# Widening in four float16 products in the convolution steps, one float32 strip buffer, and the first statistics ahead of the sign weights

## Chip, cores and metric

The kernel runs on one core of a Trainium2 chip. The metric is device time in microseconds, from the first to the last instruction of the execution, including the little around it. All products run on TensorE (PE), elementwise work on VectorE (DVE), ScalarE (ACT) and GpSimd (POOL); SyncE (SP) issues the transfers.

## What is computed

The input is 32 images of 64 channels and 112x112 pixels, float32. Two layers follow each other; each adds to x the result of a branch whose input is a group normalisation of x (32 groups of 2 channels, no affine part):

```python
# layer 0
x = x + conv3x3(group_norm(x), sign(weight) * alpha)        # 64 -> 64 channels
# layer 1
h = einsum('oc,bchw->bohw', w_in, group_norm(x))            # widening, 64 -> 256 channels
f = rfft2(patches_8x8(h)) * fft_filt;  h = irfft2(f)        # filter in each 8x8 patch
h = depthwise_conv3x3(h, w_dw)
x1, x2 = split(h, 2)                                        # 128 channels each
x = x + einsum('oc,bchw->bohw', w_out, gelu(x1) * x2)
```

## The kernel before

**Tiling.** Two images form a pair and fill the 128 partitions (2 x 64 channels), so there are 16 pairs. A pair is cut into 14 strips of 8 rows. A strip has 14 patches of 8x8, taken two at a time as 7 blocks of 16 columns (`NBLK`). The blocks are worked on in the four groups of `GROUPS`, (0,2), (2,4), (4,6) and (6,7): groups 0 to 2 have two blocks, group 3 has one.

**Layer 1, a strip.** `normalise_patches` (ACT) makes `xn`; `transposed` (PE) and `pixels` (ACT) make `xT`; `forward_transform` (PE) takes the patches to their spectrum, and `spectrum` (ACT) puts it back into the same buffer (`xf = xT`, float32). `widened` (PE) multiplies each block's spectrum with `win_sb` into two PSUM banks, in float32: four 64x64 quadrants a block, 256 columns each. `filtered` (DVE) multiplies by the filter into `hf`. `evaluated` (PE, float32) takes `hf` to 121 nodes of a short convolution scheme, `weighted` (DVE) multiplies by the taps into `v32`. `high_nodes` (ACT) rounds `v32` to float16 (`v_hi`), `low_nodes` (GpSimd) makes the remainder `v_lo` in float16, and `interpolated` (PE, float16) sums both into `Y`. `gelu`, `carried0`, `gated`, `keep0` and `keep1` finish the rows, `projected` (PE) multiplies by `w_out`, and `lifted` (ACT) and `residual` (GpSimd) add it to x.

**Layer 0, a strip.** `stats_x` (DVE) takes the statistics. Once they are complete, `strip32` (ACT) writes the normalised strip in float32 to `n32`, `strip16` (ACT) writes it again in float16 to `S_hi`, a ring of four strips, and `low_strip` (GpSimd) subtracts both into `S_lo`. `convolution` (PE, float16) needs the strips j-1 to j+1 and runs 9 taps x 2 parts x 4 quadrants for half a strip each. `convolved` (DVE) adds the result to x and `stats_1` takes the statistics for layer 1.

**Order.** All five queues are written out by hand in `image(n, ...)`, over 14 steps t. Step t brings the front of strip t (patches, transform, spectrum), widening to nodes of strip t-1, interpolation of strip t-2 and projection of strip t-3, all of pair n, while layer 0 of pair n+1 runs in between: its statistics in steps 0 to 4, its strips' normalisation as `NORM_STEPS` says (strip 0 in step 5, two strips in each of steps 6 to 11, one in step 12), and two convolutions in each of steps 6 to 12. Steps 6 to 12 are the "convolution steps" and have an order of their own; the others are "plain". `kind(b, s)` tells for a strip s of pair b which of the two orders its middle part meets; it is "conv" for strips 5 to 11 of each pair but the last, so in 15 x 7 = 105 cases. In a convolution step `widened` is issued for the groups 1, 3, 0 and 2 (`HF_ORDER`). Before the first `image` the layer 0 of the first pair runs alone: statistics, all 14 strips, all 14 convolutions.

**Waits.** Engines meet at counting semaphores. Those that matter here: `pool_slo` counts finished `low_strip`, and convolution j waits for j+2 of the pair; `pe_conv` counts convolutions, and a slot of the ring is written for strip j once convolution j-3 is done (`act.wait_ge(pe_conv, n * STRIPS + j - RING_STRIPS + 2)`); `act_xf` counts finished `spectrum`; `pool_vlo` guards the four slots of `v32`. In a convolution step ScalarE's queue has, in this order: `gelu` of image 0, `lifted` 0, `strip32(a)`, `keep0`, `lifted` 1, `strip16(a)`, `strip32(b)`, `strip16(b)`, `high_nodes` of image 0, group 3, and so on. GpSimd's has `low_strip(a)`, `residual` 0, `low_nodes(0, 3)`, `low_strip(b)`, `residual` 1, the three other `low_nodes` of image 0, then the four of image 1. Here a and b are the two strips of `NORM_STEPS[t]`. Before, `strip32` takes one of two buffers and waits for the `low_strip` of two strips earlier:

```python
if j >= 2 or not first:
    act.wait_ge(pool_slo, n * STRIPS + j - 1 if j >= 2 else n * STRIPS)
```

Of the kernel before, what the change touches and what calls it, by code (L numbers as in the profile page):

```python
# [8 lines left out]
ALU = mybir.AluOpType  # L9
# [85 lines left out]
def build(nc, x, conv_w, alpha, w_in, w_dw, filt, w_out, forward, pick, pair, identity, nodes, taps, ext, out):  # L95
# [34 lines left out]
    with ctx:  # L130
# [12 lines left out]
        win_sb = sb("win_sb", [128, C2])  # L143
        wout_sb = sb("wout_sb", [HC, C])
# [10 lines left out]
        xf = xT  # L155
        hf = sb("hf", [BPX, IMGS, NBLK, C2])
        v32 = sb("v32", [128, 4, 2, 2, C2])
# [61 lines left out]
        dve_conv = sem("dve_conv")  # L219
        dve_hf = sem("dve_hf")  # L220
# [41 lines left out]
        def kind(b, s):  # L262

            last = isinstance(b, int) and b == PAIRS - 1
            return "conv" if CONV_FROM <= (s + MID) % STRIPS <= CONV_TO and not last else "plain"

# [52 lines left out]
        def _(pool):  # L319
# [13 lines left out]
            def low_strip(n, j):  # L333
                row = j % RING_STRIPS * ROWS
                pool.wait_ge(act_shi, n * STRIPS + j + 1)
                nc.gpsimd.tensor_tensor(S_lo[:, row:row + ROWS, 1:1 + W], n32[:, j % 2],  # L336
                                        S_hi[:, row:row + ROWS, 1:1 + W], ALU.subtract).then_inc(pool_slo, 1)

            def low_nodes(b, s, img, grp):
# [3 lines left out]
                nc.gpsimd.tensor_tensor(v_lo[:, img, :, k0:k1, :], v32[:, V_ORDER[kind(b, s)][img].index(grp), :, 0:k1 - k0, :],  # L343
# [9 lines left out]
            def image(n, par, prev, front, more):  # L353
                for t in range(STRIPS if front else OUT):
                    mid = item(n, t, MID, prev, front)
                    done = item(n, t, OUT, prev, front)
                    if more and CONV_FROM <= t <= CONV_TO:
# [19 lines left out]
                    else:  # L377
# [10 lines left out]
                        if mid:  # L388
# [24 lines left out]
        def _(act):  # L413
            def strip32(n, par, j, first):

                if j == 0:
                    act.wait_ge(dve_grpx, n * 4 + 4)
                if j >= 2 or not first:
                    act.wait_ge(pool_slo, n * STRIPS + j - 1 if j >= 2 else n * STRIPS)
                nc.scalar.activation(n32[:, j % 2], X[par][:, j * ROWS:(j + 1) * ROWS, :], ACT.Identity, bias=nbx[:],  # L420
                                     scale=rstdx[:])

            def strip16(n, par, j, first):

                row = j % RING_STRIPS * ROWS
# [4 lines left out]
                nc.scalar.activation(S_hi[:, row:row + ROWS, 1:1 + W], X[par][:, j * ROWS:(j + 1) * ROWS, :], ACT.Identity,  # L430
                                     bias=nbx[:], scale=rstdx[:]).then_inc(act_shi, 1)
# [10 lines left out]
            def pixels(n, s, bank):  # L442
                act.wait_ge(pe_xT, n * STRIPS + s + 1)
                if n or s:
                    act.wait_ge(pe_hf, 4 * (n * STRIPS + s))
                nc.scalar.activation(xT[:].rearrange("p k c -> p (k c)"), flat(bank, NBLK * 128), ACT.Copy).then_inc(act_xT, 1)  # L446
# [7 lines left out]

            def high_nodes(b, s, img, grp):
# [6 lines left out]
                nc.scalar.activation(v_hi[:, img, :, k0:k1, :], v32[:, V_ORDER[kind(b, s)][img].index(grp), :, 0:k1 - k0, :],  # L462
# [30 lines left out]
            def image(n, par, prev, front, more):  # L493
                for t in range(STRIPS if front else OUT):
# [3 lines left out]
                    if more and CONV_FROM <= t <= CONV_TO:  # L498
# [4 lines left out]
                        if more and len(NORM_STEPS.get(t, ())) > 0:  # L503
                            strip32(n + 1, 1 - par, NORM_STEPS[t][0], False)
# [35 lines left out]
                    else:  # L540
# [20 lines left out]
                        if front:  # L561
                            spectrum(n, t, BANK_P)
                        if mid:
                            high_nodes(mid[0], mid[1], 1, 3)
                        if more and len(NORM_STEPS.get(t, ())) > 0:
                            strip32(n + 1, 1 - par, NORM_STEPS[t][0], False)
                            strip16(n + 1, 1 - par, NORM_STEPS[t][0], False)
# [14 lines left out]
            act.wait_ge(pool_zero, N_ZERO)  # L582
            for j in range(STRIPS):
                strip32(0, 0, j, True)
                strip16(0, 0, j, True)
# [8 lines left out]
        def _(dve):  # L594
# [72 lines left out]
            def weighted(b, s, img, grp, bank):  # L667
# [3 lines left out]
                    v32[:, V_ORDER[kind(b, s)][img].index(grp), :, 0:k1 - k0, :],  # L671
# [26 lines left out]
            def image(n, par, prev, front, more):  # L698
                for t in range(STRIPS if front else OUT):
# [9 lines left out]
                    if more and CONV_FROM <= t <= CONV_TO:  # L709
# [4 lines left out]
                        if mid:  # L714
# [3 lines left out]
                            if before:  # L718
                                dve.wait_ge(pool_vlo[1], 4 * i - 3)
                            weighted(b, s, 0, 3, BANK_Q)  # L720
                            if before:
                                dve.wait_ge(pool_vlo[1], 4 * i - 2)
                            weighted(b, s, 0, 0, BANK_P)
                            if before:
                                dve.wait_ge(pool_vlo[1], 4 * i - 1)
# [3 lines left out]
                        if mid:  # L729
                            if before:  # L730
                                dve.wait_ge(pool_vlo[1], 4 * i)
# [7 lines left out]
                        if mid:  # L739
                            dve.wait_ge(pool_vlo[0], 4 * i + 1)  # L740
# [3 lines left out]
                        if mid:  # L744
                            dve.wait_ge(pool_vlo[0], 4 * i + 2)
# [3 lines left out]
                        if mid:  # L749
                            dve.wait_ge(pool_vlo[0], 4 * i + 3)  # L750
# [3 lines left out]
                        if mid:  # L754
                            dve.wait_ge(pool_vlo[0], 4 * i + 4)
                            weighted(b, s, 1, 0, BANK_P)
                    else:
# [16 lines left out]
                        if mid:  # L774
                            if before:
                                dve.wait_ge(pool_vlo[1], 4 * i - 3)
                            weighted(b, s, 0, 3, BANK_P)
                            if before:
                                dve.wait_ge(pool_vlo[1], 4 * i - 2)
# [5 lines left out]
                        if mid:  # L785
                            if before:
                                dve.wait_ge(pool_vlo[1], 4 * i - 1)
# [427 lines left out]
```

## Time and profile before

| | |
|---|---|
| median of 3 runs | 5393.75 us (5391.17 to 5396.26) |
| the profiled execution, its own time | 5396.35 us |
| its span | 5394.6 us |
| granted TensorE clock, mean | 0.997 |
| busy: PE, DVE, POOL, ACT | 97%, 86%, 79%, 65% |
| PE weight loads | 57% |
| DMA queues | about 11% of 16 engines |

The profile is of one execution. Busy shares are means over two kinds of step, so they are only a first hint; rows of a timeline give an instruction's start and length in microseconds, and in brackets how long the engine was idle before it and which instruction released it. "x40" is a run of 40 records of one kind; a float32 product has two records, a float16 product one. Rows of the chain name the work that held up the end, one after the other. ACT and DVE rows overlap by some 0.1 us, since the next instruction starts before the last one's end is recorded.

### The profile page before, as it was taken

What the parts mean: (1) busy time and instruction counts of PE and PEld (TensorE: products, weight loads), DVE (VectorE), ACT (ScalarE), POOL (GpSimd) and SP (SyncE); (2) the same over time, 40 slices, a digit from 0 to 9 for tenths busy, and PEclk for the clock granted to TensorE, in tenths of its full rate; (3) what the DMA queues carried; (4) which work ended last, traced back from release to release, by engine and by line L of the source; (5) the groups of instructions that cost most, each with busy time, mean ns of one, the idle gap of its engine ahead of it and who ended that gap; (6) DMA issues with size and microseconds to landing.
All of it is one profiled execution on the core that took longest, in us unless ns stands there. A gap on an engine that the chain in (4) does not pass through costs nothing.

```text
span 5394.6 us, 200882 instructions
## 1 busy us (share of the span) xinstructions
PE 5249.1 (97%) x88932; PEld 3061.1 (57%) x88932; DVE 4631.7 (86%) x5701; ACT 3526.7 (65%) x4642; POOL 4236.2 (79%) x2503
## 2 busy tenths in 40 slices
PE   5999999999999999999999999999999999999998
PEld 4555555555555555555555555555555555555554
DVE  6889888898888888888898888988889888898886
ACT  3666666666666666666666676666666667666665
POOL 3878778787887877878778787887878878787787
PEclk9999999999999999999999999999999999999999
DMA  2011010110101101010010100101011110110000
GB/s 103 19 50 43 37 45 28 54 40 37 54 22 50 43 37 53 19 58 35 37 53 28 51 33 38 55 36 43 33 50 40 39 41 33 50 43 20 23 26 26
DMA packets 43804, 219.20 MB, mean 41 GB/s; under 512 B 5350, under 2 KB 5960, under 8 KB 36808
## 3 DMA queue, kind: packets, MB, share of 16 engines
q1 hardware_dynamic: 42952, 206.36, 9.9%
q8 instruction: 716, 11.73, 0.9%
q14 instruction: 136, 1.11, 0.1%
HBM read 103.58 MB, written 102.76 MB: 38 GB/s over the span
## 4 chain that ended last, share of the span: by engine, by line
PE 86%; DVE 10%; issue 3%; DMA 0%; ACT 0%; POOL 0%; DVEq 0%; SPq 0%; POOLq 0%; ACTq 0%
PE PS L913 28%; PE PS L931 21%; PE PS L873 14%; PE PS L901 12%; PE PS L945 7%; DVE v L670 5%; PE PS L882 4%; DVE hf L663 3%; DVE bn L601 1%; DVE g L695 1%; DVE PS L679 0%; DVE PS L686 0%; DMA alpha_sb<-in_alpha 0%; POOL v_lo L343 0%; PE PS L847 0%
## 5 line engine op out<-in xcount | busy, mean ns | idle before, releaser
L343 POOL TENSOR_TENSOR v_lo<-v,v_hi 128x1024 f16<-128x1024 f32 (+1 forms) x1792 | 3357.5, 1898 | 841.9 <-ACT v_hi L462 834.5
L462 ACT ACTIVATE v_hi<-v 128x1024 f16<-128x1024 f32 (+1 forms) x1792 | 1647.0, 944 | 902.4 <-DVE v L670 532.6
L670 DVE TENSOR_TENSOR v<-PS,smul 128x1024 f32<-128x1024 f32 (+1 forms) x1792 | 1909.8, 1086 | 288.6 <-PE PS L913 271.0
L913 PE MATMUL PS<-hf,c_nodes 64*64 64x512 f32 (+1 forms) x14336 | 1661.8, 556 | 25.7 <-DVE v L670 4.5
L931 PEld LDWEIGHTS PS<-c_ext,v_hi 128*128 128x128 f16 x14336 | 1129.9, 97 | 541.2 <-issue 198.5
L931 PE MATMUL PS<-c_ext,v_hi 128*128 128x100 f16 (+2 forms) x14336 | 1258.6, 203 | 5.2 <-ACT gel L482 3.8
L931 PE MATMUL PS<-c_ext,v_lo 128*128 128x100 f16 (+2 forms) x14336 | 1250.2, 202 | 0.0
L931 PEld LDWEIGHTS PS<-c_ext,v_lo 128*128 128x128 f16 x14336 | 1118.0, 97 | 1.2
L663 DVE TENSOR_TENSOR hf<-PS,mult 128x1024 f32<-128x1024 f32 (+1 forms) x896 | 955.0, 1086 | 117.5 <-PE PS L901 101.0
L901 PE MATMUL PS<-win_sb,xT 64*64 64x256 f32 x12544 | 824.9, 388 | 48.0 <-DVE hf L663 28.9
L873 PE MATMUL PS<-S_hi,csign 64*64 64x448 f16 (+2 forms) x8640 | 746.4, 336 | 9.2 <-POOL S_lo L336 9.2
L873 PE MATMUL PS<-S_lo,csign 64*64 64x448 f16 (+2 forms) x8640 | 747.5, 337 | 0.0
L913 PEld LDWEIGHTS PS<-hf,c_nodes 64*64 64x64 f32 x14336 | 407.9, 131 | 583.1 <-DVE v L670 157.0
L901 PEld LDWEIGHTS PS<-win_sb,xT 64*64 64x64 f32 x12544 | 413.7, 132 | 394.3 <-DVE hf L663 160.5
L446 ACT ACTIVATE xT<-PS 128x896 f32<-128x896 f32 x224 | 205.6, 918 | 650.0 <-PE PS L882 650.0
L336 POOL TENSOR_TENSOR S_lo<-n,S_hi 128x896 f16<-128x896 f32 x224 | 411.5, 1837 | 214.6 <-ACT S_hi L430 214.6
L695 DVE TENSOR_TENSOR g<-PS,gel 128x912 f32<-128x912 f32 (+1 forms) x448 | 496.3, 1108 | 58.9 <-DVE PS L686 1.9
L482 ACT ACTIVATE gel<-PS 128x912 f32<-128x912 f32 (+1 forms) x448 | 413.6, 923 | 116.6 <-DVE PS L679 115.6
L945 PE MATMUL PS<-g,wout_sb 128*64 128x448 f32 (+2 forms) x1792 | 445.6, 574 | 7.7 <-DVE g L695 5.9
L873 PEld LDWEIGHTS PS<-S_hi,csign 64*64 64x64 f16 x8640 | 314.1, 107 | 142.8 <-DVE v L670 28.5
L873 PEld LDWEIGHTS PS<-S_lo,csign 64*64 64x64 f16 x8640 | 314.6, 106 | 135.2 <-issue 32.1
L469 ACT ACTIVATE g<-PS 128x448 f32<-128x448 f32 (+1 forms) x448 | 244.7, 546 | 81.3 <-PE PS L945 79.3
(68 smaller groups left out, 4143.2 us busy)
## 6 DMA issues: line engine op xcount, KB each, us to landing
out_x<-Xa SPq DMA_DIRECT2D x96, 448.0 KB, 2.6
out_x<-Xb SPq DMA_DIRECT2D x96, 448.0 KB, 2.5
Xa<-in_x SPq DMA_DIRECT2D x8, 2240.0 KB, 9.0
Xb<-in_x SPq DMA_DIRECT2D x8, 2240.0 KB, 8.9
Xa<-in_x SPq DMA_DIRECT2D x8, 1792.0 KB, 7.0
Xb<-in_x SPq DMA_DIRECT2D x8, 1792.0 KB, 7.2
Xa<-in_x SPq DMA_DIRECT2D x8, 1344.0 KB, 6.0
Xb<-in_x SPq DMA_DIRECT2D x8, 1344.0 KB, 6.4
```

The source lines that it names most:

```text
L336: nc.gpsimd.tensor_tensor(S_lo[:, row:row + ROWS, 1:1 + W], n32[:, j % 2], S_hi[:, row:row + ROWS, 1:1 + W], ALU.subtract).then_inc(pool_s ...
L343: nc.gpsimd.tensor_tensor(v_lo[:, img, :, k0:k1, :], v32[:, V_ORDER[kind(b, s)][img].index(grp), :, 0:k1 - k0, :], v_hi[:, img, :, k0:k1, ...
L462: nc.scalar.activation(v_hi[:, img, :, k0:k1, :], v32[:, V_ORDER[kind(b, s)][img].index(grp), :, 0:k1 - k0, :], ACT.Copy).then_inc(act_vhi ...
L482: nc.scalar.activation(gel[:, :, r0:r1, :], Y[:, :, r0:r1, :], ACT.Gelu).then_inc(act_y0, 1)
L663: nc.vector.tensor_tensor(hf[:, :, k0:k1, :], PS[:, bank:bank + 2, 0:(k1 - k0) * C2].rearrange("p i (k c) -> p i k c", c=C2), mult[:].unsq ...
L670: nc.vector.tensor_tensor(v32[:, V_ORDER[kind(b, s)][img].index(grp), :, 0:k1 - k0, :], PS[:, bank:bank + 2, 0:(k1 - k0) * C2].rearrange(" ...
L695: nc.vector.tensor_tensor(g[:, img, r0:r1, :].rearrange("p r (b c) -> p b r c", c=YC), Y[:, :, r0:r1, :], gel[:, :, r0:r1, :], ALU.mult).t ...
L873: last = nc.tensor.matmul(PS[c * C:(c + 1) * C, bank + h, i0 * W:(i0 + m) * W], csign[r * C:(r + 1) * C, tap, :], S[r * C:(r + 1) * C, row ...
L901: last = nc.tensor.matmul(PS[side * P * P:(side + 1) * P * P, bank + r, (k - k0) * C2:(k - k0 + 1) * C2], xf[r * C:(r + 1) * C, k, side * ...
L913: last = nc.tensor.matmul(PS[points, bank + side, 0:(k1 - k0) * C2], c_nodes[half, points], hf[half, img, k0:k1, :].rearrange("p k c -> p ...
L931: last = nc.tensor.matmul(Y[:, b0, :, col - b0 * YC:end - b0 * YC], v[:, img, patch % 2, patch // 2, half * HC:(half + 1) * HC], c_ext[:, ...
L945: last = nc.tensor.matmul(Z[img * C:(img + 1) * C, 0:(r1 - r0) * HALF_W], wout_sb[:], g[:, img, r0:r1, 1 + q * HALF_W:1 + (q + 1) * HALF_W ...
```

## The change

1. **Widening in convolution steps.** In strips of kind "conv", `spectrum_high` (ACT) rounds the spectrum to float16 right behind `spectrum`, and `spectrum_low` (GpSimd) subtracts it into `xf_lo`. `widened` then uses four float16 products (high x high, low x high, high x low, low x low) that accumulate in PSUM, each with 64 rows (one image) and all 128 columns, 256 columns of result, where it had four float32 quadrants a block. It waits for `pool_xl` in place of `act_xf`. `win_hi` and `win_lo` are made once at the start. In plain steps nothing changes here, except that plain step 5 makes the spectrum of strip 5, which is of kind "conv".
2. **One strip buffer.** `n32` has one slot. `strip16` comes before `strip32` everywhere, and `strip32` waits for the `low_strip` of the strip just before.
3. **Buffers of the nodes.** `v32` has three slots for the groups 0 to 2 and `v31` one small slot of each image for group 3; the counts waited for come from `lows_before`. They are the same numbers as before.
4. **The start.** The statistics of strips 0 to 10 of the first pair stand before the wait for the sign weights, those of 11 to 13 behind it. A small activation into `nb1`, which is overwritten later, runs on ScalarE first.

```diff
-        n32 = sb("n32", [128, 2, ROWS, W])
+        n32 = sb("n32", [128, ROWS, W])
...
+            def spectrum_low(n, s):
+                pool.wait_ge(act_xh, xl_count(n, s + 1))
+                nc.gpsimd.tensor_tensor(xf_lo[:], xf[:], xf_hi[:], ALU.subtract).then_inc(pool_xl, 1)
...
@@ gpsimd, convolution step @@
                             low_nodes(mid[0], mid[1], 0, 2)
+                        if front and kind(n, t) == "conv":
+                            spectrum_low(n, t)
                         if mid:
                             low_nodes(mid[0], mid[1], 1, 3)
@@ gpsimd, plain step @@
                             low_nodes(mid[0], mid[1], 1, 3)
+                        if front and kind(n, t) == "conv":
+                            spectrum_low(n, t)
                         if mid:
                             low_nodes(mid[0], mid[1], 1, 0)
...
@@ scalar @@
             def strip32(n, par, j, first):
+                if j or not first:
+                    act.wait_ge(pool_slo, n * STRIPS + j)
+                nc.scalar.activation(n32[:], X[par][:, j * ROWS:(j + 1) * ROWS, :], ACT.Identity, bias=nbx[:],
+                                     scale=rstdx[:]).then_inc(act_shi, 1)
...
+            def spectrum_high(n, s):
+                i = n * STRIPS + s
+                act.wait_ge(act_xf, i + 1)
+                if i:
+                    act.wait_ge(pe_hf, 4 * i)
+                nc.scalar.activation(xf_hi[:], xf[:], ACT.Copy).then_inc(act_xh, 1)
...
@@ scalar, convolution step @@
-                            strip32(n + 1, 1 - par, NORM_STEPS[t][0], False)
+                            strip16(n + 1, 1 - par, NORM_STEPS[t][0], False)
                         if up:
                             keep0(up[0], up[1], 0)
                         if done:
                             lifted(done[0], done[1], 1)
                         if more and len(NORM_STEPS.get(t, ())) > 0:
-                            strip16(n + 1, 1 - par, NORM_STEPS[t][0], False)
+                            strip32(n + 1, 1 - par, NORM_STEPS[t][0], False)
                         if more and len(NORM_STEPS.get(t, ())) > 1:
+                            strip16(n + 1, 1 - par, NORM_STEPS[t][1], False)
                             strip32(n + 1, 1 - par, NORM_STEPS[t][1], False)
-                            strip16(n + 1, 1 - par, NORM_STEPS[t][1], False)
...
                         if front:
                             spectrum(n, t, BANK_P)
+                            if kind(n, t) == "conv":
+                                spectrum_high(n, t)
...
+            nc.scalar.activation(nb1[:], m_half[:], ACT.Identity)
...
@@ vector, start @@
+            for j in range(STRIPS - 3):
+                stats_x(0, 0, j)
             dve.wait_ge(dma_conv, 16 * N_CONV)
...
-            for j in range(STRIPS):
+            for j in range(STRIPS - 3, STRIPS):
                 stats_x(0, 0, j)
             channels_x(0)
...
+            nc.vector.tensor_copy(win_hi[:], win_sb[:]).then_inc(dve_prep, 1)
+            dve.wait_ge(dve_prep, 3)
+            nc.vector.tensor_tensor(win_lo[:], win_sb[:], win_hi[:], ALU.subtract).then_inc(dve_prep, 1)
...
@@ tensor, widened @@
+                    pe.wait_ge(pool_xl, xl_count(b, s + 1))
+                    for k in range(k0, k1):
+                        for part, (x16, win) in enumerate(((xf_hi, win_hi), (xf_lo, win_hi), (xf_hi, win_lo), (xf_lo, win_lo))):
+                            for r in range(IMGS):
+                                last = nc.tensor.matmul(PS[:, bank + r, (k - k0) * C2:(k - k0 + 1) * C2],
+                                                        x16[r * C:(r + 1) * C, k, :], win[r * C:(r + 1) * C, :],
+                                                        start=part == 0, stop=part == 3)
```

## Rows read from the trace of the kernel before

**Rows 1.** The page: engines' busy time, chain by engine, one group's weight loads.
```profile
PE 5249.1 (97%) x88932; PEld 3061.1 (57%) x88932; DVE 4631.7 (86%) x5701; ACT 3526.7 (65%) x4642; POOL 4236.2 (79%) x2503
...
PE 86%; DVE 10%; issue 3%; DMA 0%; ACT 0%; POOL 0%; DVEq 0%; SPq 0%; POOLq 0%; ACTq 0%
...
L931 PEld LDWEIGHTS PS<-c_ext,v_hi 128*128 128x128 f16 x14336 | 1129.9, 97 | 541.2 <-issue 198.5
```

**Rows 2.** The chain, 2281 to 2309 us: start, length (us), what.
```profile
2283.17 1.38 PE PS L931 x32
2284.55 2.50 PE PS L901 x40
...
2292.93 6.87 PE PS L873 x144
```

**Rows 3.** Timeline, TensorE: start, length (us), instruction, idle time before.
```profile
2285.95 0.64 PEld L901 LDWEIGHTS PS<-win_sb,xT 64*64 64x64 f32 x16 [0.41 <-DVE hf L663]
...
2292.76 0.37 PE L873 MATMUL PS<-S_hi,csign 64*64 64x448 f16 x4
```

**Rows 4.** Timeline of VectorE, same step.
```profile
2296.40 0.68 DVE L644 SCALAR_TENSOR_TENSOR Xb<-PS,alpha_sb,Xb 128x448 f32<-128x448 f32 x1 [1.66 <-PE PS L873]
```

**Rows 5.** Timeline of ScalarE, same step.
```profile
2288.46 1.12 ACT L430 ACTIVATE S_hi<-Xb,nbx,rstdx 128x896 f16<-128x896 f32 x1
2289.48 1.12 ACT L420 ACTIVATE n<-Xb,nbx,rstdx 128x896 f32<-128x896 f32 x1
...
2292.01 1.58 ACT L462 ACTIVATE v_hi<-v 128x512 f16<-128x512 f32 x2 [0.38 <-PE PS L931]
...
2306.03 1.58 ACT L462 ACTIVATE v_hi<-v 128x512 f16<-128x512 f32 x2 [1.54 <-PE PS L931]
```

**Rows 6.** Timeline of GpSimd, same step.
```profile
2280.01 7.55 POOL L343 TENSOR_TENSOR v_lo<-v,v_hi 128x512 f16<-128x512 f32 x4 [1.90 <-ACT v_hi L462]
2289.66 1.84 POOL L336 TENSOR_TENSOR S_lo<-n,S_hi 128x896 f16<-128x896 f32 x1 [2.10 <-ACT S_hi L430]
...
2292.72 1.16 POOL L343 TENSOR_TENSOR v_lo<-v,v_hi 128x512 f16<-128x512 f32 x1 [0.21 <-ACT v_hi L462]
2293.84 1.83 POOL L336 TENSOR_TENSOR S_lo<-n,S_hi 128x896 f16<-128x896 f32 x1
```

**Rows 7.** Timeline of GpSimd, steps 5 and 6 of the same pair.
```profile
2192.66 7.46 POOL L343 TENSOR_TENSOR v_lo<-v,v_hi 128x1024 f16<-128x1024 f32 x4 [1.43 <-ACT v_hi L462]
2201.39 2.14 POOL L343 TENSOR_TENSOR v_lo<-v,v_hi 128x1024 f16<-128x1024 f32 x1 [1.26 <-ACT v_hi L462]
...
2205.27 4.25 POOL L343 TENSOR_TENSOR v_lo<-v,v_hi 128x1024 f16<-128x1024 f32 x2
```

**Rows 8.** Timeline of TensorE, step 6.
```profile
2201.59 1.09 PE L901 MATMUL PS<-win_sb,xT 64*64 64x256 f32 x16 [1.18 <-DVE v L670]
...
2212.27 0.37 PE L873 MATMUL PS<-S_hi,csign 64*64 64x448 f16 x4
```

**Rows 9.** The chain of the first 150 us.
```profile
4.58 15.73 DMA alpha_sb<-in_alpha
...
21.29 14.77 DVE bn L601 x28
...
40.11 1.28 ACT L420
...
45.69 1.84 POOL S_lo L336
...
47.67 50.11 PE PS L873 x980
```

**Rows 10.** Timeline of SyncE's queue, the four loads of the first pair.
```profile
0.74 1.89 SPq L276 DMA_DIRECT2D Xa<-in_x  x4
```

**Rows 11.** DMA issues, first 60 us: first and last of these four, us to landing.
```profile
Xa<-in_x SPq DMA_DIRECT2D x1, 2240.0 KB, 8.2
...
Xa<-in_x SPq DMA_DIRECT2D x1, 1344.0 KB, 17.4
```

More of the change, by code:

```diff
@@ L265, in kind, with xl_count, kind_after, nodes32 @@
             return "conv" if CONV_FROM <= (s + MID) % STRIPS <= CONV_TO and not last else "plain"
+        def xl_count(b, s):
+            return (STRIPS // 2) * b + min(max(s - CONV_FROM + MID, 0), STRIPS // 2) if b < PAIRS - 1 else (STRIPS // 2) * b
+        def kind_after(b, s):
+            return kind(b, s + 1) if s < STRIPS - 1 else kind(b + 1, 0)
+        def nodes32(b, s, img, grp):
+            if grp == 3:
+                return v31[:]
+            return v32[:, [other for other in V_ORDER[kind(b, s)][img] if other != 3].index(grp)]
+        def lows_before(b, s, img, grp):
+            if img == 0:
+                b, s = (b, s - 1) if s else (b - 1, STRIPS - 1)
+            mine, theirs = V_ORDER[kind(b, s) if img else kind_after(b, s)][img], V_ORDER[kind(b, s)][1 - img]
+            if grp == 3:
+                at = theirs.index(3)
+            else:
+                at = theirs.index([other for other in theirs if other != 3][[other for other in mine if other != 3].index(grp)])
+            return 4 * (b * STRIPS + s) + at + 1
         def conv_strips(t):
@@ L335, in low_strip @@
                 pool.wait_ge(act_shi, n * STRIPS + j + 1)
-                nc.gpsimd.tensor_tensor(S_lo[:, row:row + ROWS, 1:1 + W], n32[:, j % 2],
+                nc.gpsimd.tensor_tensor(S_lo[:, row:row + ROWS, 1:1 + W], n32[:],
                                         S_hi[:, row:row + ROWS, 1:1 + W], ALU.subtract).then_inc(pool_slo, 1)
+            def spectrum_low(n, s):
+                pool.wait_ge(act_xh, xl_count(n, s + 1))
+                nc.gpsimd.tensor_tensor(xf_lo[:], xf[:], xf_hi[:], ALU.subtract).then_inc(pool_xl, 1)
             def low_nodes(b, s, img, grp):
@@ L414, in strip32, with strip16 @@
             def strip32(n, par, j, first):
+                if j or not first:
+                    act.wait_ge(pool_slo, n * STRIPS + j)
+                nc.scalar.activation(n32[:], X[par][:, j * ROWS:(j + 1) * ROWS, :], ACT.Identity, bias=nbx[:],
+                                     scale=rstdx[:]).then_inc(act_shi, 1)
+            def strip16(n, par, j, first):
+                row = j % RING_STRIPS * ROWS
                 if j == 0:
                     act.wait_ge(dve_grpx, n * 4 + 4)
[L418 to L425, printed above, removed]
                 if j >= RING_STRIPS:
@@ L461, in high_nodes @@
                     act.wait_ge(pe_y, 4 * i - 2 + 2 * img)
-                nc.scalar.activation(v_hi[:, img, :, k0:k1, :], v32[:, V_ORDER[kind(b, s)][img].index(grp), :, 0:k1 - k0, :],
+                nc.scalar.activation(v_hi[:, img, :, k0:k1, :], nodes32(b, s, img, grp),
                                      ACT.Copy).then_inc(act_vhi[img], 1)
@@ L562, in image @@
                             spectrum(n, t, BANK_P)
+                            if kind(n, t) == "conv":
+                                spectrum_high(n, t)
                         if mid:
@@ L897, in widened @@
                 k0, k1 = GROUPS[grp]
-                pe.wait_ge(act_xf, b * STRIPS + s + 1)
-                for k in range(k0, k1):
-                    for r, side in ((0, 0), (1, 1), (0, 1), (1, 0)):
-                        last = nc.tensor.matmul(PS[side * P * P:(side + 1) * P * P, bank + r, (k - k0) * C2:(k - k0 + 1) * C2],
-                                                xf[r * C:(r + 1) * C, k, side * P * P:(side + 1) * P * P],
-                                                win_sb[r * C:(r + 1) * C, :], start=True, stop=True)
+                if kind(b, s) == "plain":
+                    pe.wait_ge(act_xf, b * STRIPS + s + 1)
+                    for k in range(k0, k1):
+                        for r, side in ((0, 0), (1, 1), (0, 1), (1, 0)):
+                            last = nc.tensor.matmul(PS[side * P * P:(side + 1) * P * P, bank + r, (k - k0) * C2:(k - k0 + 1) * C2],
+                                                    xf[r * C:(r + 1) * C, k, side * P * P:(side + 1) * P * P],
+                                                    win_sb[r * C:(r + 1) * C, :], start=True, stop=True)
+                else:
+                    pe.wait_ge(pool_xl, xl_count(b, s + 1))
+                    for k in range(k0, k1):
+                        for part, (x16, win) in enumerate(((xf_hi, win_hi), (xf_lo, win_hi), (xf_hi, win_lo), (xf_lo, win_lo))):
[3 more added lines that the diff above has]
+                                                        start=part == 0, stop=part == 3)
                 last.then_inc(pe_hf, 1)
```

55 lines of the change are left out of this document (32 added, 23 removed).

## Prediction

> **What bounds the kernel now.** I read the page first: the tensor engine is busy 97% of the span, and the chain that ended last is 86% tensor engine and 10% vector engine [rows 1]. Such a share says nothing yet of one stage, so I then read the chain and the timelines of one convolution step (image pair 6, 2282 to 2309 us). Below I call the groups of the widening W1, W3, W0 and W2 in the order in which a convolution step issues them, and the two strips that a step normalises a and b.
>
> The chain of that step [rows 2] shows three things. The float32 widening of five blocks takes 2.50 us, 0.50 a block. The float16 convolution takes 6.87 us for 144 products, 36 sets of four 64x64 quadrants, 0.19 us a set of 448 columns. That is one set at the pace of one stream (448 columns at 2.4 GHz are 0.187): quadrants with different rows, and quadrants with the same columns and another bank, run beside each other, and the loads cost nothing. The float16 interpolation needs 1.38 us for 32 products with 128x128 weights, 43 ns for a load and a product. So the engine streams nearly without a gap, and what it is given less to do is worth something, unless another engine holds it at that place. Two places are close. W2 begins at 2285.95 and its loads waited for the vector engine's result of W3 [rows 3]. The second convolution of the step begins at 2292.76 + 3.43 = 2296.19 [rows 2, 3], and it needs the low half of strip b, which GpSimd finishes at 2293.84 + 1.83 = 2295.67 [rows 6]: half a microsecond of room.
>
> **The widening itself.** Seven convolution steps in each of 15 pairs, 105 in all, change. Before: seven blocks at 0.50. After: four products of 256 columns for each half of the rows, the halves beside each other. By the conv's rate a pair of streams costs 256/448 of 0.19, which is 0.109 us, and four of them 0.44 a block. Half of the array's rows with all 128 columns is a shape of which the trace has no fast example. From below, 4 x 256 columns at 2.4 GHz are 0.427. From above, nothing beside anything, it is 0.85. I take 0.44, since the quadrants show both kinds of overlap and the 43 ns show 128-column loads hidden. That saves about 0.05 a block. W1 gives 0.10, W3 0.05, which moves the vector engine's filtered W3 and with it W2 by 0.15; W2 gives 0.10 more. So the first projection and all behind it come 0.25 us earlier, not 7 x 0.06 = 0.4, since W0 is done before W2 may start.
>
> The Trainium skill ("TensorE: Matmul & The Clock Gate", Part 3, the mechanism) says that a weight load overlaps products in flight only when its row group differs. By it each of the four rounds would show its load, and the kernel would be slower; the 43 ns above, all on the same rows, speak against it, and it is a rival below.
>
> **Added on ScalarE and GpSimd.** spectrum_high: a 128x896 activation costs at most the 1.12 us of the strip's. It comes behind spectrum, where ScalarE sat idle 1.54 us before v_hi [rows 5]: hidden. spectrum_low: 128x896, float32 less float16, like a strip's 1.84 us [rows 6]. In a convolution step GpSimd was idle 1.90 us before low_nodes(1,3) at 2280.01. It can begin about 1.0 us after spectrum's end, so 1.84 of work in the rest of that gap pushes low_nodes(1,3) by 0.5. Behind it wait four v_lo (7.55 us, to 2287.56) and then low_strip(a), which before waited until 2289.66 [rows 6]: 2.1 us of cover. The vector engine wants these buffers in the next step only: hidden.
>
> **One strip buffer.** strip16(a) takes the place of strip32(a) and the reverse, so low_strip(a) starts when it did. But strip32(b) must now wait for it. From the start of strip32(a), which stands where S_hi stood at 2288.46 [rows 5], I add: 1.12 and 0.08 to GpSimd's start (2289.66), 1.84, a hand-over of 0.07 (an estimate, a little under the 0.08 of the other way), then 1.02 (as from 2288.46 to 2289.48) until ScalarE takes v_hi for group 3, 0.71 from there to GpSimd (2292.01 to 2292.72), 1.12 to the next strip (2292.72 to 2293.84), 1.83, and 0.14 to the tensor engine (45.69 + 1.84 to 47.67). The sum is 7.93 and ends at 2296.39 [rows 5, 6, 9]. The second convolution stood ready at 2296.19, so it would now wait 0.20. (The vector engine's [1.66] wait at 2296.40 [rows 4] is for the first convolution; it has time.) Both sides start 0.25 earlier. A step with two strips so gains 0.25 - 0.20 = 0.05. Bounds: 0.25 where the chain fits, a loss of 0.2 where hand-overs are 0.1 dearer and the widening saves half. Step 12 has one strip and gains the full 0.25.
>
> **The first convolution step of each pair.** The spectrum of strip 5 is made in plain step 5, and its low half is queued behind low_nodes(1,3). That ends at 2192.66 + 7.46 = 2200.12, and GpSimd was idle only 1.26 us until 2201.39 [rows 7]. So spectrum_low runs 2200.12 to 2201.95. W1 waits for it: 2202.05 in place of 2201.59 [rows 8]. low_nodes(1,0) ends 2204.07, low_strip(0) 2205.85, two v_lo (4.2) 2210.05, low_strip(1) 2211.9. Now the single buffer: strip32(2) from 2211.95, v_hi 2212.97, v_lo 2213.68, low_strip(2) 2214.80 to 2216.63, second convolution 2216.77. Before it stood at 2212.27 + 3.43 = 2215.70 [rows 8]. That is 1.07 us late, with the widening's gain swallowed. GpSimd catches up soon after, in idle time like the 1.90 us of [rows 6], so this happens once a pair. Bounds 0.6 to 1.3, by the same hand-overs.
>
> Per pair: 5 x 0.05 + 0.25 - 1.07 = -0.57, which is 8.6 us lost over 15 pairs.
>
> **The start.** The sign weights' work waits until 20.3 us, and the 28 statistics (14.77 us, 1.055 a strip) stand behind it, to 36.06 [rows 9]. The four loads were issued from 0.74 to 2.6 [rows 10] and landed 8.2 to 17.4 us after issue [rows 11]. After: 11 strips from 8.9 to 20.5, sign weights 0.95, three strips 3.2, to 24.6: 11.4 us earlier. The other copies for the filter weights (128x256 each) lie beside the tensor engine's group sums: nothing. The new small activation on ScalarE draws the 1.28 us table load out of the chain [rows 9]. Against it: the first two strips in one buffer are 1.02 + 1.12 + 0.08 + 1.84 + 0.07 + 1.12 + 0.08 + 1.84 + 0.14 = 7.3 us instead of 47.67 - 41.39 = 6.3. And from strip 4 a slot of the ring comes free only when convolution j-2 is done. Then strip16, strip32 and the low half follow, some 4.35 us with the hand-overs, while a convolution takes 3.43 [rows 2]; before, strip32 was ahead, and 3.2 fitted. Convolution j waits for j-2's end + 4.35, so every second one waits 0.9: five, 4.5 us. Sum: -11.4 - 1.3 + 1.0 + 4.5 = -7.2 us, from -9 to -4.
>
> **The sum.** 5394.6 + 8.6 - 7.2 = 5396.0 of span. The profiled execution took 1.75 more than its span and 2.6 more than the median of the three runs, so the forecast is 5395 us. Its own range is 5383 to 5405.
>
> **Rivals.** A, faster: the chain of the single buffer is a little shorter than summed, the convolution never waits for strip b, and blocks cost 0.43. Then 90 steps give 0.3 (27 us), the first step of a pair loses 0.8 (12), the start gives 7: 5372. For it: 0.2 us decides it. Against: every hand-over summed comes from a row. It decides once each two-strip step gains 0.18 instead of 0.05.
> B, slower: the same chain is dearer, as ScalarE takes strip32(b) late and keep1, v_hi and the second strip pile up behind it. At 0.3 us a step in 75 steps: 5395 + 22 = 5417. It decides from 0.13 a step on. For it: four queued instructions are now in series, and each may slip. Against: ScalarE has idle time left, 1.54 us at one place of the step alone [rows 5].
> C, slower by far: the row halves do not run together, 0.85 a block: 0.35 x 7 x 105 = 257 us, 5650. A second way to nearly the same end is that loads are shown: 97 ns of a float16 load [rows 1] and 107 of stream, four times, are 0.82 a block, 0.32 x 735 blocks = 235 us, 5630. This is the skill's rule named above (its section gives no other price here); 43 ns a pair [rows 2] is against it.
>
> **Chances.** Forecast 0.44, A 0.24, B 0.25, C 0.07. 0.2% (11 us) is about what a measurement can tell from no change. Faster 0.24, same 0.44, slower 0.32. The range, 5371 to 5428, takes in A and B and leaves out C and some of the tails.
>
> **What would show it.** Five blocks of widening at 2.2 us in place of 2.5. A wait of the second convolution for S_lo, 0.2 us in most convolution steps and near 1 us in the first of a pair. GpSimd's spectrum_low at 1.84 with W1 of the first step waiting for it. The statistics ending near 24.6 us, the first convolution near 36. I am wrong if a block costs more than 0.5, if no wait for S_lo shows, or if the filtered group 3 no longer gates W2.

## The result and the profile after

| | before | after |
|---|---|---|
| median of 12 runs each | 5393.86 us (5391.17 to 5396.26) | 5406.49 us (5402.29 to 5412.72) |
| profiled execution, own time | 5396.35 us | 5403.27 us |
| its span | 5394.6 us | 5401.2 us |
| PE, DVE, POOL, ACT busy | 97%, 86%, 79%, 65% | 97%, 86%, 82%, 67% |

The ratio is 1.0023, with an interval of 1.0014 to 1.0032: 12.6 us more by the medians. The forecast was 5395, its own range 5383 to 5405, the whole range 5371 to 5428. So the time lies just outside the forecast's own range, toward rival B, inside the whole one.

The page of after: engines' busy time, the chain by engine, and one costly group (out<-in, count | busy us, mean ns | idle before, releaser). They answer to [rows 1].

```profile
PE 5248.3 (97%) x88932; PEld 3131.2 (58%) x88932; DVE 4632.7 (86%) x5703; ACT 3616.6 (67%) x4748; POOL 4425.2 (82%) x2608
...
PE 79%; DVE 10%; POOL 7%; issue 3%; ACT 1%; DMA 0%; DVEq 0%; POOLq 0%
...
L367 POOL TENSOR_TENSOR S_lo<-n,S_hi 128x896 f16<-128x896 f32 x224 | 410.3, 1832 | 158.4 <-ACT n L456 158.4
```

The tensor engine is as busy as before to 1 us in 5248. What is new is GpSimd with 7% of the chain, where [rows 1] has 0%, and its 189 us more of work, in 105 more instructions. Where it enters is seen in the waits of TensorE over the whole span (line, releaser: us in total, times, longest). The first row was there before. In the place of the second before had 15 waits for the vector engine's v, 17.7 us; in the place of the third only the one wait at the start, which is the longest here.

```profile
PE PS L959 <- DVE hf L715: 28.8, 87, 0.3
PE PS L967 <- POOL xf_lo L372: 25.6, 15, 1.7
PE PS L930 <- POOL S_lo L367: 20.0, 21, 8.9
```

**A step with two strips.** The chain of after in image pair 5, 1896 to 1914 us (start, length, what), answers to [rows 2]: two blocks of W1, the interpolation, the five blocks of W3 and W2, the convolutions.

```profile
1896.40 1.01 PE PS L967 x16
1897.41 1.38 PE PS L997 x32
1898.79 2.38 PE PS L967 x40
...
1907.05 7.05 PE PS L930 x140
```

The five blocks took 2.38 us where they took 2.50. The timeline of the loads (PEld) and of the vector engine shows how the 2.38 comes about. The first two rows are one pair of halves after another, the third is the first load behind a change of shape, the fourth W2's first load; the last is the vector engine's filtered group 3.

```profile
1896.48 0.10 PEld L967 LDWEIGHTS PS<-win_lo,xf_hi 64*128 64x128 f16 x2
1896.59 0.10 PEld L967 LDWEIGHTS PS<-win_lo,xf_lo 64*128 64x128 f16 x2
...
1897.34 0.10 PEld L997 LDWEIGHTS PS<-c_ext,v_hi 128*128 128x128 f16 x1 [0.21 <-issue]
...
1900.12 0.10 PEld L967 LDWEIGHTS PS<-win_hi,xf_hi 64*128 64x128 f16 x2 [0.20 <-DVE hf L715]
```
```profile
1899.37 0.69 DVE L715 TENSOR_TENSOR hf<-PS,mult 128x512 f32<-128x512 f32 x1
```

A pair of halves came every 0.11 us (1896.48, 1896.59, and so on to 1897.03), so a block is 0.44, as forecast. The loads of 0.10 lie under the products, although every one goes to rows on which a product is in flight. But from the last pair of W1 at 1897.13 to the interpolation's first product at 1897.34 it is 0.21, so 0.10 goes at the change of shape. And W2's first load waits for the vector engine's result of W3, as in [rows 3].

The wait that the single buffer brings is seen in three queues. ScalarE, the second strip32:

```profile
1902.58 1.12 ACT L456 ACTIVATE n<-Xa,nbx,rstdx 128x896 f32<-128x896 f32 x1
1903.60 1.12 ACT L468 ACTIVATE S_hi<-Xa,nbx,rstdx 128x896 f16<-128x896 f32 x1
1905.64 1.13 ACT L456 ACTIVATE n<-Xa,nbx,rstdx 128x896 f32<-128x896 f32 x1 [0.92 <-POOL S_lo L367]
```

GpSimd, same step; these answer to [rows 6]:

```profile
1893.11 1.90 POOL L372 TENSOR_TENSOR xf_lo<-xT,xf_hi 128x896 f16<-128x896 f32 x1 [0.71 <-ACT xf_hi L500]
1894.96 7.46 POOL L378 TENSOR_TENSOR v_lo<-v,v_hi 128x512 f16<-128x512 f32 x4
1903.78 1.83 POOL L367 TENSOR_TENSOR S_lo<-n,S_hi 128x896 f16<-128x896 f32 x1 [1.36 <-ACT n L456]
...
1907.37 1.16 POOL L378 TENSOR_TENSOR v_lo<-v,v_hi 128x512 f16<-128x512 f32 x1 [0.75 <-ACT v_hi L509]
1908.49 1.83 POOL L367 TENSOR_TENSOR S_lo<-n,S_hi 128x896 f16<-128x896 f32 x1
```

TensorE, the last set of the first convolution and the first of the second:

```profile
1910.11 0.37 PE L930 MATMUL PS<-S_lo,csign 64*64 64x448 f16 x4
1910.47 0.39 PE L930 MATMUL PS<-S_hi,csign 64*64 64x448 f16 x4
```

spectrum_low took 1.90 and was hidden: GpSimd still had 1.36 us idle before low_strip(a). From low_strip(a) at 1903.78 the chain strip32, v_hi, v_lo, low_strip(b) ends at 1910.32, and the second convolution begins 0.14 later, at 1910.47. The sets come every 0.19; this one came after 0.36, so TensorE lost 0.17, and both convolutions took 7.05 in place of 6.87 [rows 2].

**The first convolution step of a pair.** The chain of after, 1861 to 1884 us, is GpSimd almost from end to end:

```profile
1861.85 5.31 POOL v_lo L378 x3
1867.16 1.84 POOL xf_lo L372
1869.01 2.10 POOL v_lo L378
1871.10 1.79 POOL S_lo L367
1872.89 4.19 POOL v_lo L378 x2
1877.09 1.80 POOL S_lo L367
...
1880.64 1.16 POOL v_lo L378
1881.80 1.80 POOL S_lo L367
1883.74 3.62 PE PS L930 x72
```

This is the sequence that the prediction added up, in the same order. W1 waited [1.71 <-POOL xf_lo L372] in place of 1.18 [rows 8].

**The start.** The chain of after, 0 to 100 us, against [rows 9]:

```profile
8.86 11.68 DVE bn L653 x22
...
21.40 3.18 DVE bn L653 x6
...
35.87 9.79 PE PS L930 x140
45.69 1.14 ACT S_hi L468
46.82 1.03 ACT n L456
47.92 1.84 POOL S_lo L367
49.90 3.66 PE PS L930 x72
```

The statistics ended at 24.58, the first convolution began at 35.87. Then the chain strip16, strip32, low half, convolution repeats five times, with a period of 7.9 us for two convolutions that took 6.86 before. Layer 0 of the first pair ended 5.8 us earlier than before (its statistics' aggregate at 95.30, before 101.11).

**Where the time went.** A pair's period, from one rstdx on GpSimd to the next, cut at the low_strip of strip a; medians over the pairs in us. Each column ends at a strip a, so the wait of a step's second convolution counts in the column behind it. Sum is that of the columns; start is the shift of the second pair's rstdx against before.

| kernel | to a of step 6 | to a of step 7 | 4 steps, to step 11 | to step 12 | rest | sum | start |
|---|---|---|---|---|---|---|---|
| before | 22.13 | 26.41 | 106.89 | 26.73 | 149.12 | 331.28 | 0 |
| after | 22.65 | 26.74 | 107.02 | 26.76 | 149.10 | 332.27 | -5.8 |

So a pair costs 0.99 us more, 0.85 of it around step 6, and 0.03 in each other step with two strips. Fifteen pairs and the start are 14.9 - 5.8 = +9.1 us. The two profiled executions differ by 6.9, those of the run repeated below by 9.9, the medians by 12.6 and 10.2. Between the 9.1 and the 6.9 stands the last pair, for which neither kernel widens in float16: from its rstd to the end before took 343.97 us and after 341.42. 0.7 of the 2.5 us are a pause in before, as described at the end. The other 1.8 lie in its last 20 us, where TensorE has little left to do and waits for other engines: the granted clock was 0.50 there in before, its lower level, and 0.67 in the last 20 us of after, and the last two interpolations of 32 products kept TensorE busy for 2.51 us each in before and 1.45 in after. The products there are the same in both kernels.

### The profile page after: what moved, and what is told of

It is laid out like the page before. It is cut to its first block, busy times and chain, and to the rows that moved or that the text cites. A ratio compares the mean times of both kernels' runs of the same rounds, so it can differ in the third digit from the quotient of the medians.

```text
span 5401.2 us, 201199 instructions
## 1 busy us (share of the span) xinstructions
PE 5248.3 (97%) x88932; PEld 3131.2 (58%) x88932; DVE 4632.7 (86%) x5703; ACT 3616.6 (67%) x4748; POOL 4425.2 (82%) x2608
## 4 chain that ended last, share of the span: by engine, by line
PE 79%; DVE 10%; POOL 7%; issue 3%; ACT 1%; DMA 0%; DVEq 0%; POOLq 0%
PE PS L979 26%; PE PS L997 20%; PE PS L930 13%; PE PS L1011 6%; PE PS L967 6%; PE PS L959 5%; POOL v_lo L378 4%; DVE v L722 4%; PE PS L939 4%; DVE hf L715 3%; POOL S_lo L367 2%; DVE bn L653 1%; DVE g L747 1%; POOL xf_lo L372 1%; ACT v_hi L509 0%
## 5 line engine op out<-in xcount | busy, mean ns | idle before, releaser
L959 PE MATMUL PS<-win_sb,xT 64*64 64x256 f32 x6664 | 439.7, 389 | 30.1 <-DVE hf L715 28.8
L959 PEld LDWEIGHTS PS<-win_sb,xT 64*64 64x64 f32 x6664 | 219.4, 133 | 192.7 <-DVE hf L715 117.6
```

The source lines that it names most:

```text
L959: last = nc.tensor.matmul(PS[side * P * P:(side + 1) * P * P, bank + r, (k - k0) * C2:(k - k0 + 1) * C2], xf[r * C:(r + 1) * C, k, side * ...
```

## The experiments

The first four kernels ran on one chip with 22 runs of before (median 5394.69), the other four on another with 21 (5396.95).

**start_only.** Before, with the new start alone.

```diff
             act.wait_ge(pool_zero, N_ZERO)
+            nc.scalar.activation(nb1[:], m_half[:], ACT.Identity)
...
+            for j in range(STRIPS - 3):
+                stats_x(0, 0, j)
             dve.wait_ge(dma_conv, 16 * N_CONV)
...
-            for j in range(STRIPS):
+            for j in range(STRIPS - 3, STRIPS):
                 stats_x(0, 0, j)
```

> The kernel before with only the edits to the start: statistics of strips 0 to 10 ahead of the wait for the sign weights, and the small activation first on ScalarE. Theory: the statistics end 11.4 us earlier and the 1.28 us table load leaves the chain, nothing behind takes it back, since both strip buffers are there: 12.7 us less, 5381 us. Rival: what the changed kernel shows at its start, 5.8 us less at the end of the layer 0 of the first pair, is all that the start can give whatever the buffers: 5388 us.

Measured: 5382.81 us (10 runs), ratio 0.9979 (0.9969 to 0.9988), 11.9 us less. The first convolution began at 34.65 and the second pair's rstdx came 13.2 us earlier; the sum of a pair's columns is 331.31, as in before. So the reordering by itself gains 12 us, twice what the start gains in after.

**one_buffer.** Before, with the single float32 buffer and strip16 ahead of strip32, everything else as it was.

```diff
-        n32 = sb("n32", [128, 2, ROWS, W])
+        n32 = sb("n32", [128, ROWS, W])
...
             def strip32(n, par, j, first):
+                if j or not first:
+                    act.wait_ge(pool_slo, n * STRIPS + j)
...
-                            strip32(n + 1, 1 - par, NORM_STEPS[t][0], False)
+                            strip16(n + 1, 1 - par, NORM_STEPS[t][0], False)
```

> The kernel before with only the single strip buffer and strip16 ahead of strip32. Theory: at the start 6.9 us more (the changed kernel gained 5.8 there in place of 12.7); in the 75 convolution steps with two strips, from the second step of a pair on, the second convolution waits 0.2 us for its strip, 15 us; in the first step of a pair 0.5, 7.5 us: 5423 us. Rival: the wait in the changed kernel comes from GpSimd's load with the spectrum's low half, and one buffer alone costs only the 6.9 us at the start: 5401 us.

Measured: 5425.15 us (5 runs), ratio 1.0059 (1.0046 to 1.0071), 30.5 us more. ScalarE shows the wait, and the chain shows both convolutions:

```profile
1945.14 1.13 ACT L417 ACTIVATE n<-Xa,nbx,rstdx 128x896 f32<-128x896 f32 x1 [0.92 <-POOL S_lo L336]
```
```profile
1946.54 7.05 PE PS L872 x143
```

The wait and the 7.05 are those of after, without one new instruction. The step takes 26.91 (before 26.72), a pair 1.47 more, and the start 6.1 more: 22 + 6. This one edit costs more than the whole change.

**two_buffers.** After, with the second float32 buffer given back. The two halves of the float16 spectrum take as many bytes as that buffer did (3584 in each partition). Here they share one place with it, since the spectrum is dead while strip b is made; added waits on pe_hf and pool_slo, not shown in the cut, guard the place, and strip32 goes first again.

```diff
-        n32 = sb("n32", [128, ROWS, W])
+        n32 = [sb("n32", [128, ROWS, W]), sb("n32b", [128, ROWS, W])]
...
-        xf_hi = sb("xf_hi", [128, NBLK, BPX], F16)
-        xf_lo = sb("xf_lo", [128, NBLK, BPX], F16)
+        half16 = n32[1][:].rearrange("p a b -> p (a b)")
+        xf_hi = half16[:, 0:NPX // 2].bitcast(F16).rearrange("p (k c) -> p k c", c=BPX)
+        xf_lo = half16[:, NPX // 2:NPX].bitcast(F16).rearrange("p (k c) -> p k c", c=BPX)
```

> The changed kernel with two strip buffers and strip32 ahead of strip16 again; the second buffer shares its place with the float16 spectrum, which is dead while the buffer is used. Theory: the widening's 0.17 us a step comes through in 90 steps (15.3 us), the start gains 12.7, the first convolution step of a pair still loses about 0.4 (6 us), since the spectrum's low half keeps GpSimd and the first widening waits for it: 5372 us. Rival: the float16 widening gives nothing by itself, the tensor engine is held by the vector engine at the nodes: start and first step alone, 5387 us.

Measured: 5377.83 us (7 runs), ratio 0.9968 (0.9957 to 0.9980): 16.9 less than before, where after was 12.6 more. ScalarE runs strip a, strip b without a wait, and the chain has the convolutions at their old length:

```profile
1914.25 1.12 ACT L477 ACTIVATE S_hi<-Xa,nbx,rstdx 128x896 f16<-128x896 f32 x1
1915.27 1.12 ACT L467 ACTIVATE n32b<-Xa,nbx,rstdx 128x896 f32<-128x896 f32 x1
```
```profile
1918.72 6.86 PE PS L940 x141
```

The step takes 26.56. With before 26.72, one_buffer 26.91 and after 26.75 the two edits add up to the digit: the widening gives 0.16 alone and 0.16 beside the single buffer. The time lies 6 us above what was expected; the step and the sum of the columns (330.70, so 0.58 less a pair) don't, and this profile has the most of the pauses named at the end: 12.1 us of them in 13 pairs, where before has 6.3.

**first_float32.** After, with the spectrum of strip 5, the one that the first convolution step widens, left in float32.

```diff
-                        if front and kind(n, t) == "conv":
+                        if front and kind(n, t) == "conv" and t >= CONV_FROM:
                             spectrum_low(n, t)
...
-                if kind(b, s) == "plain":
+                if kind(b, s) == "plain" or s < CONV_FROM:
```

> The changed kernel, but the widening of strip 5, the first of a pair that meets a convolution step, stays in float32, so plain step 5 has no spectrum_low and 90 strips are widened in float16, not 105. Theory: the late second strip in the first convolution step shrinks from 1.0 us to about 0.5, 7.5 us less than the changed kernel, a ratio of about 1.001 to the kernel before. Rival: the whole 1.0 us goes or none of it: 12 us less, or as the changed kernel.

Measured: 5397.36 us (11 runs), ratio 1.0005 (0.9996 to 1.0014). Column one of the table returns to 22.13, column two stays at 26.74: the queued spectrum_low costs 0.52 of the first step, and the other 0.33 is the single buffer (0.48 in one_buffer) less the 0.16 of the widening.

**two_buffers_first_float32.** Both of the last two edits in one kernel.

> Both mends at once: two strip buffers as in two_buffers, and the first strip of a pair that meets a convolution step widened in float32. Theory: the start gains 12.7 us, 90 steps gain the 0.16 us that two_buffers showed (26.56 us a step for 26.72), 14.4 us, and the first convolution step is as before, since GpSimd has no spectrum_low ahead of it: 5394.7 - 27 = 5368 us, 6 us under two_buffers by the step and 10 by the median. Rival: the irregular pauses of TensorE grow with what the queues hold, and the median stays at 5375 or above.

Measured: 5370.13 us (5 runs), ratio 0.9951 (0.9938 to 0.9965), 26.8 less than before: the fastest of the kernels that keep all four products. The rival's 5375 or more did not come. W1 of the first step waits as in [rows 8] again, and both convolutions take 6.87:

```profile
1855.25 1.09 PE L969 MATMUL PS<-win_sb,xT 64*64 64x256 f32 x16 [1.18 <-DVE v L732]
```
```profile
1892.65 6.87 PE PS L940 x144
```

**two_products.** After, with two of the four products. It leaves out the two with the low half of the filter weights.

```diff
-                        for part, (x16, win) in enumerate(((xf_hi, win_hi), (xf_lo, win_hi), (xf_hi, win_lo), (xf_lo, win_lo))):
+                        for part, (x16, win) in enumerate(((xf_hi, win_hi), (xf_lo, win_hi))):
```

> The changed kernel with only the first two of the four float16 products (high and low half of the spectrum by the high half of w_in); the two with the low half of w_in are left out. A block falls from 0.44 us to 0.22. Theory: what comes through is what W1 saves (0.44 us), since W2 starts when the filtered group 3 is done and that waits for the vector engine's carried0 behind the interpolation; the wait of the second convolution for S_lo (0.19) goes too, as its chain starts behind W2: 26.75 - 0.63 = 26.1 us a step, 90 x 0.63 = 57 us less than the changed kernel, 5350. Rivals: TensorE sets the whole step, 7 x 0.22 = 1.5 us a step, 140 us less; or GpSimd sets it, and hardly anything changes.

Measured: 5348.02 us (4 runs), ratio 0.9908 (0.9894 to 0.9921), 59 less than the repeat of after on the same chip, where 57 were expected. The step takes 26.06, 0.69 less than after. Seven blocks at 0.22 less would be 1.54: less than half of it arrives. The timeline of TensorE shows where the rest is:

```profile
1908.33 0.28 PE L967 MATMUL PS<-win_hi,xf_hi 64*128 64x256 f16 x2 [0.29 <-DVE hf L715]
...
1909.14 0.60 PE L1011 MATMUL PS<-g,wout_sb 128*64 128x448 f32 x2 [0.20 <-ACT g L516]
```

W2 waits for the vector engine's filtered W3, and behind it the projection waits for ScalarE. One part of the expectation fell: the second convolution's wait for S_lo did not go. It is 0.25 (its first set at 1892.53, the last of the first convolution at 1892.09, pace 0.19). The trace shows why: both sides of that wait moved together. Both hang on ScalarE's gelu, which waits 0.38 here for the vector engine's carried0: ScalarE runs from it to strip32(a) without a pause, and the chain up to the first convolution goes over it too. In the median of the 75 steps with two strips the first convolution begins 7.20 us behind it (in after 7.61) and strip32(a) 2.95 (in after 3.32). So the convolutions gained 0.41 and the chain to low_strip(b) 0.37.

**low_spectrum_early.** After, with spectrum_low of strip 5 ahead of low_nodes(1,3).

```diff
-                            low_nodes(mid[0], mid[1], 1, 3)
+                            pass
                         if front and kind(n, t) == "conv":
                             spectrum_low(n, t)
                         if mid:
+                            low_nodes(mid[0], mid[1], 1, 3)
                             low_nodes(mid[0], mid[1], 1, 0)
```

> The changed kernel, but in plain step 5 spectrum_low stands ahead of low_nodes(1,3) on GpSimd, not behind it. Theory: the first widening of the first convolution step no longer waits for it (0.5 us), but the second convolution stands where it did, since GpSimd's queue holds the same work before low_strip(b): the time stays that of the changed kernel within 2 us. Rival: the two waits add up, and 0.5 x 15 = 8 us go.

Measured: 5407.74 us (10 runs), ratio 1.0023 (1.0014 to 1.0032), as after's on the same chip. TensorE's wait is gone and the vector engine's, for the second convolution, has grown:

```profile
1869.83 0.28 PE L968 MATMUL PS<-win_hi,xf_hi 64*128 64x256 f16 x2 [1.19 <-DVE v L723]
```
```profile
1888.65 0.68 DVE L697 SCALAR_TENSOR_TENSOR Xa<-PS,alpha_sb,Xa 128x448 f32<-128x448 f32 x1 [1.39 <-PE PS L931]
```

In after that wait is 0.84. The 0.5 us that W1 gained were waited for behind it, at the second convolution, since GpSimd's queue ends when it did: the table's first two columns are 22.67 and 26.76. W1's wait of 1.71 was a sign of the full queue, not the cost.

**changed_again.** After once more, for a second profile beside the last three.

> The changed kernel once more, to see whether its timed runs (5402 to 5413 us) scatter again by more than those of the kernel before, beside a profile. Theory: its median comes out at 5394.7 + 12 = 5404 to 5408, and the steps in the profile keep their 26.75 us, so that the rest is irregular pauses. Rival: the profiled execution (5403) was the usual one and the median falls to 5401 to 5403.

Measured: 5407.19 us (11 runs), ratio 1.0021 (1.0012 to 1.0029), own time of the profiled execution 5406.22. The columns are 22.66, 26.76, 107.05, 26.76, 149.13. So after's first profile, at 5403.27, was one of its lower executions, as before's, at 5396.35, was one of the higher: 3.2 below and 2.5 above the medians. The columns and the start of this profile add up to 10.3 us more than before, its median is 10.2 more.

## Why the prediction came out as it did

**The block: right.** 0.11 us a pair of halves and 0.44 a block, as worked out from the convolution's pace and the 43 ns. Rival C has nothing in the trace. By the rule that it took up, of the Trainium skill ("TensorE: Matmul & The Clock Gate", Part 3, the mechanism), each of the four rounds would have shown its load; here a load of 0.10 on rows on which a product is in flight is covered whole.

**The gain of a step: the step of the prediction that failed.** It gave W1 0.10, W3 0.05 and W2 0.10, 0.25 in all. The first projection came 0.17 earlier (4.74 behind W1's start, before 4.91), and the table has 0.16. The gate by the filtered group 3 was there as said. What was missing is the 0.10 us that the engine loses when it goes from the 64x128 shape to the interpolation's and from W2 to the projection. The two float16 blocks of W1 are 0.88 and took 0.98 up to the interpolation's first product; the float32 ones, at 0.50 a block, took 1.03 and so had only 0.03 of it. two_products has the same loss, 0.55 us for four pairs of 0.11. So W1 and W2 gave 0.05 each in place of 0.10, and W3 gave 0.07 where 0.05 were forecast. The loss counts in each step from 7 on; steps 8 to 12 show it as 5 x 0.08 x 15 = 6 us, and in step 7 it is nearly made up by a first step that cost a little less than summed (below).

**The wait for the single buffer: right, in place and size.** 0.20 was forecast from hand-overs, 0.17 to 0.19 measured, in after and in one_buffer alike. With the smaller gain a step with two strips is 0.03 dearer where it was to be 0.05 cheaper. Over steps 8 to 12 that lifts the pair's loss from 0.57 to 0.97; measured is 0.99. B's sign and some of its size came true, but not by its mechanism: no hand-over was dearer.

**The first step of a pair: right.** In the prediction's terms its cost is 1.07 less the 0.25 of the step behind it, 0.82 up to a of step 7; measured are 0.52 + 0.33 = 0.85, and as the gain was 0.17 its own cost was 1.02. first_float32 and one_buffer split it, low_spectrum_early shows that GpSimd's queue sets it.

**The start: right in parts, 1.4 us short in sum.** Statistics' end and first convolution came as worked out (24.6 and 36, measured 24.58 and 35.87). The five waits are 1.03 each, not 0.9: 5.1 instead of 4.5. And the first convolution itself took 6.39 us in place of 5.48, since it ran longer at the slow pace that the last section shows. -11.8 + 0.9 + 5.1 = -5.8, where the forecast had -7.2. The reordering is worth 12 us by itself, and the single buffer takes 7 of them back (two_buffers' start is 12.9 us early).

**The sum.** By steps +9.1 in place of +1.3: 6.3 from the pairs and 1.4 from the start. By medians the parts are: start -11.9 (start_only), single buffer +30.5 (one_buffer), widening -5.0 (two_buffers less start_only). They add up to +13.6; measured are 12.6 and 10.2. The widening's -5.0 holds the cost of its GpSimd work in the first step; without that (two_buffers_first_float32 and start_only, each against before on its own chip) it is -14.9. On the second chip the columns account for the median (10.3 and 10.2). For the first result 3.5 us stay open between the 9.1 of its columns and the 12.6 of its medians; differences by execution (first convolution, pauses, the clock in the last 20 us) are of that size, but the other executions have no trace. That the time fell within the wide range owes something to luck: the sum is the rest of two larger terms that nearly cancel, and the pair's term was short by more than a third.

## What to carry to other kernels

Where a change frees room for a faster operation by halving a buffer, price the buffer first, by a sum of hand-overs along both queues up to the consumer: here 30 us for the buffer stand against 5 for the operation, or 15 where its work on the full queue of the first step is left out. A gain on a full engine must be followed to the next instruction that another engine releases, and a block's pace is not its cost until the change of shape behind it is counted. When a new instruction on a shared queue shows as a wait at one place, moving it ahead helps only if the queue has slack up to the last of its consumers.

## What the runs showed of the chip

**A slow first convolution, by a length that varies.** The granted clock of the window 35.87 to 41 us reads 1.00, yet the sets of the first convolution begin at twice the later distance. Timeline of TensorE in after:

```profile
35.87 0.59 PE L930 MATMUL PS<-S_hi,csign 64*64 64x448 f16 x4 [8.86 <-POOL S_lo L367]
...
40.73 0.76 PE L930 MATMUL PS<-S_lo,csign 64*64 64x448 f16 x4
41.10 0.63 PE L930 MATMUL PS<-S_hi,csign 64*64 64x448 f16 x4
41.47 0.45 PE L930 MATMUL PS<-S_lo,csign 64*64 64x448 f16 x4
```

0.37 from set to set is 448 columns at 1.2 GHz; behind 41.47 it is 0.19, the same at 2.4 GHz. TensorE had been idle for 8.86 us ahead of it. In before the fast pace began 3.7 us behind the first product, here 5.6. From its first product to the vector engine's first read of it the first convolution took 5.48 in before, 5.17 in start_only, 5.10 in two_buffers, 6.39 in after, 6.13 in changed_again and 6.58 in two_buffers_first_float32. The last and two_buffers have the same start, so the length is a matter of the execution, worth up to 1.5 us of the few that this study is about. What sets it was not found.

**Pauses of TensorE without a releaser.** In all kernels the mean of the four-step column lies above its median, by 0.25 us in before, 0.28 in after, 0.34 in changed_again, 0.44 in two_buffers. Behind it are single pauses, and most of them return at the same product of the program. Timeline of TensorE in before, after and changed_again, the same product of the same pair:

```profile
3502.46 0.34 PE L891 MATMUL PS<-c_fwd,xT 64*64 64x64 f32 x6 [1.21 <-issue]
```
```profile
3506.14 0.34 PE L948 MATMUL PS<-c_fwd,xT 64*64 64x64 f32 x6 [1.15 <-issue]
```
```profile
3507.61 0.34 PE L948 MATMUL PS<-c_fwd,xT 64*64 64x64 f32 x6 [1.15 <-issue]
```

Another one falls into the 16 records that before begins at 2305.97 and that take 2.67 us where their like take 1.95; after and changed_again pause in the same 16, for longer (idle 0.49 and 0.51 at one product). Laid against the median of 13 pairs product by product, pauses over 0.25 us add up to 6.3 us in before, 7.2 in after, 8.2 in changed_again and 12.1 in two_buffers. So the places belong mostly to the program, and the length, or whether a pause comes at all, to the execution. The DMA engines were busy 87% of 2303.0 to 2306.5 in before, up to the pause there, but only 37% of 3498.0 to 3501.3, up to the one shown; that transfers cause them was not tried. Their cause was not found.
